# A graph-attention layer on one Trainium2 core: adjacency loads of 2 MB in four buffers instead of 1 MB in six, and TensorE packing whole tiles behind each step's other work

## What is computed

```python
x   = normal(8192, 256)                       # float32
adj = bernoulli(0.000488281, (8192, 8192))    # int32
h = maximum(layernorm(x), 0)
support = (h @ weight)                        # 4 heads of 64
f1, f2  = einsum(support, weight_u), einsum(support, weight_v)
scores  = leaky_relu(f1[None, :] + f2[:, None], 0.2) * adj     # 0 where there is no edge
attn    = softmax over the nonzero entries of a row
out     = x + attn @ support + bias + h @ proj_w.T + proj_b
```

## Time and profile before

| what | value |
|---|---|
| time, median of 3 runs | 862.98 us (861.75 to 863.88) |
| time of the profiled execution | 860.12 us |
| its span, first to last instruction | 858.4 us |
| busy PE, PEld, DVE, ACT, POOL | 83%, 51%, 75%, 15%, 62% |
| DMA traffic | 329.82 MB, mean 384 GB/s |
| of it adjacency | 256 transfers of 1024 KB, median 13.3 us from issue to landing |
| of it gathers | 384, median 6.2 us from issue to landing |
| chain that ended last | PE 42%, DMA 25%, DVE 24% |

### The profile page before, as it was taken

How to read it: one execution, slowest core, us unless ns; L and a number is a source line. 1 busy time by engine, 2 the same in 40 slices (tenths; PEclk the granted TensorE clock), 3 DMA queues, 4 the chain that set the end, 5 groups by cost and what they waited for, 6 DMA issues and landing times.

```text
span 858.4 us, 11157 instructions
## 1 busy us (share of the span) xinstructions
PE 710.9 (83%) x3011; PEld 434.2 (51%) x3011; DVE 643.1 (75%) x2740; ACT 129.3 (15%) x467; POOL 529.0 (62%) x598
## 2 busy tenths in 40 slices
PE   2989999999956878887888888788888878888865
PEld 0656666666513545454555445354544445454454
DVE  4556666657446988879869798977979787886887
ACT  0223333333210111000001011000011100000010
POOL 4344455454467776667766667676766766676570
PEclk9999999999966989888879898887989888988789
DMA  9999999999999999999999999999999999999971
GB/s 307 422 407 393 416 422 416 407 423 413 419 410 384 385 401 402 388 405 384 402 393 374 399 374 405 383 404 384 390 396 375 406 366 400 359 403 401 397 302 53
DMA packets 63855, 329.82 MB, mean 384 GB/s; under 512 B 12795, under 2 KB 15560, under 8 KB 31024
## 3 DMA queue, kind: packets, MB, share of 16 engines
q1 hardware_dynamic: 43056, 286.28, 83.8%
q0 software_dynamic: 18432, 34.30, 11.1%
q10 hardware_dynamic: 2304, 8.52, 2.4%
HBM read 328.99 MB, written 16.91 MB: 403 GB/s over the span
## 4 chain that ended last, share of the span: by engine, by line
PE 42%; DMA 25%; DVE 24%; issue 4%; POOL 3%; ACT 1%; POOLq 0%; ACTq 0%; SPq 0%
DMA adj_raw<-in_adj 21%; PE ps_words L400 11%; PE ps_agg L461 9%; PE ps_agg L381 7%; PE ps_two L381 6%; DVE att L933 5%; PE ps_two L400 5%; DVE cand L787 3%; DVE base L943 3%; POOL att L717 2%; DMA att<-support_table,idx 2%; PE ps_score L445 2%; DMA att<-in_x 1%; PE ps_words L392 1%; DMA support_table<-att 1%
## 5 line engine op out<-in xcount | busy, mean ns | idle before, releaser
L717 POOL DMA_INDIRECT att<-support_table,idx x384 | 417.4, 1087 | 188.7 <-issue 105.8
L400 PE MATMUL ps_words<-adj_raw,pack_w 128*128 128x512 fp8e4 x640 | 186.7, 428 | 25.4 <-DMA adj_raw<-in_adj 25.3
L461 PE MATMUL ps_agg<-att,ident 128*128 128x260 f32 x640 | 176.3, 428 | 8.5 <-DVE att L933 8.5
L461 PEld LDWEIGHTS ps_agg<-att,ident 128*128 128x128 f32 x640 | 135.1, 218 | 41.6 <-issue 18.6
L400 PE MATMUL ps_two<-adj_raw,pack_w 128*128 128x512 fp8e4 x384 | 118.9, 457 | 24.6 <-DMA adj_raw<-in_adj 24.5
L400 PEld LDWEIGHTS ps_words<-adj_raw,pack_w 128*128 128x128 bf16 x640 | 62.1, 106 | 125.3 <-DMA adj_raw<-in_adj 39.8
L787 DVE MAX8 cand<-ps_words 128x8 f32<-128x128 f32 x320 | 67.1, 281 | 66.3 <-PE ps_words L400 66.3
L933 DVE TENSOR_TENSOR att<-att 128x1536 f32<-128x1536 f32 x64 | 109.4, 1750 | 0.4 <-ACT att L625 0.4
L708 POOL COPY record<-att 128x8 f32<-128x8 f32 x64 | 13.4, 209 | 117.4 <-ACT att L569 117.4
L400 PEld LDWEIGHTS ps_two<-adj_raw,pack_w 128*128 128x128 bf16 x384 | 38.7, 113 | 91.5 <-DMA adj_raw<-in_adj 40.0
L381 PE MATMUL ps_agg<-w_all,hT 128*128 128x260 f32 x256 | 63.0, 389 | 4.1 <-ACT hT L565 4.1
(11 more groups left out here) (118 smaller groups left out, 821.2 us busy)
## 6 DMA issues: line engine op xcount, KB each, us to landing
adj_raw<-in_adj SPq DMA_DIRECT2D x256, 1024.0 KB, 13.3
support_table<-att ACTq DMA_DIRECT2D x16, 520.0 KB, 8.8
att<-in_x SPq DMA_DIRECT2D x16, 512.0 KB, 6.7
out<-base SPq DMA_DIRECT2D x15, 512.0 KB, 14.1
att<-support_table,idx POOLq DMA_INDIRECT x384, 6.2
out<-base SPq DMA_DIRECT2D x4, 128.0 KB, 1.9
w_all<-in_proj_wT SPq DMA_DIRECT2D x2, 128.0 KB, 6.0
w_all<-in_weight SPq DMA_DIRECT2D x2, 128.0 KB, 6.3
```

Of the source, the lines that this page charges most:

```text
L400: mm = nc.tensor.matmul(ps_words[buffer_of(t)][:, k * 512:(k + 1) * 512], pack_w[:, u * UT + s, :], adj_low[:, n % HELD, s, k * 512:(k + 1 ...
L461: mm = nc.tensor.matmul(ps_agg[:, b, 0:ROW], ident[:] if k < OWN else onehotT[:, g % RING, b], gathered[:, g % RING, b, k], start=(k == 0) ...
L717: pool.indirect_dma_start(gathered[:, g % RING, b, k, :], None, table, bass.IndirectOffsetOnAxis(idx[:, g % RING, b, k:k + 1], 0), bounds_ ...
```

## The change

Five things change, and all arithmetic stays.

- UNITS goes from 4 to 2 and HELD from 6 to 4. A tile's adjacency comes in two transfers of 2 MB, 16 KB in one piece for each partition, and 8 MB are held instead of 6. A unit's packing is now eight matmuls, and the buffer is freed behind the eighth.
- In the first phase the two units of a tile are packed in the second and the fourth place of a round, eight matmuls each, in place of four in each of four places.
- In a step of the second phase TensorE first runs `offsets`, `aggregate`, `edge_records`, `row_scores`, `aggregate` and `edge_refs`, and packs in one go behind them.
- It packs tile t + 2 in the step that picks t. Tile 17 is packed ahead of the first step; tile 63 keeps its place in the step behind the loop.
- To make room in SBUF, `spare`, `uv_row`, `projb_row` and `place_hi` become views of `base`, and `hT` a view of `onehot`. These are used at other times than what they now share with.

```diff
-UNITS = 4
-HELD = 6
+UNITS = 2
+HELD = 4
@@ tiles
-        spare = sb("spare", [P, 4, HF])
-        uv_tmp = spare[:].rearrange("p (q c) d -> p q c d", q=2)
+        uv_tmp = base[:, TILES - 4:].rearrange("p (q c) d -> p q c d", q=2)
+        uv_row = base[:, TILES - 6:TILES - 4]
+        projb_row = base[:, TILES - 7]
+        place_hi = base[0:2, TILES - 9:TILES - 7].rearrange("p a d -> p (a d)").bitcast(BF16)
-        hT = sb("hT", [P, 2, KC * P])
+        hT = onehot[:].rearrange("p a b m -> p a (b m)")
@@ first phase
-                    if q > 0:
-                        pack_unit(g + 1, q - 1)
+                    if q > 0 and q % (LOAD // UNITS) == 0:
+                        pack_unit(g + 1, q // (LOAD // UNITS) - 1)
@@ second phase
             pe.wait_ge(s_staged, TILES)
+            pack_places(FIRST + 1)
+            for u in range(UNITS):
+                pack_unit(FIRST + 1, u)
             for g in range(LATE):
-                new = [t + 1 for t in picks[g]]
                 offsets(g)
-                pack_places(new[0])
-                for u in range(UNITS // 2):
-                    pack_unit(new[0], u)
                 if g >= 2:
                     aggregate(g - 2, 0)
                 edge_records(g)
                 if g > 0:
                     row_scores(g - 1)
-                for u in range(UNITS // 2, UNITS):
-                    pack_unit(new[0], u)
-                if g > 0:
-                    edge_refs(g - 1)
                 if g >= 2:
                     aggregate(g - 2, 1)
-                for t in new[1:]:
-                    pack_places(t)
-                    for u in range(UNITS):
-                        pack_unit(t, u)
+                if g > 0:
+                    edge_refs(g - 1)
+                for t in picks[g]:
+                    if t + 2 < TILES - 1:
+                        pack_places(t + 2)
+                        for u in range(UNITS):
+                            pack_unit(t + 2, u)
```

## The result

| kernel | median us | lowest to highest | ratio to before [95%] |
|---|---|---|---|
| before | 863.13 (6 runs) | 858.91 to 863.88 | |
| changed | 911.23 (6 runs) | 907.81 to 915.66 | 1.0569 [1.0547, 1.0592] |

The changed kernel is 5.7% slower. The forecast was 886 us with a range up to 903: the right sign and the right cause, with half of the size. The profiled execution of the changed kernel took 915.66 us, its span is 913.8 us. So the two spans differ by 55.4 us where the medians differ by 48.1.

What follows compares the result with a forecast made beforehand. The second phase was taken as DMA-bound at 37.7 us a pair, becoming gather-paced at 39.8. 13 pairs gave +27, the start +3, the end -7: +23 us, so a median of 886 us, range 838 to 903.

Steps and rivals of the forecast that it cites:

- The mechanism: Second phase: 16 KB rows lengthen q1's turns, so a gather takes 1.95 us against 1.3 us of issue, and VectorE waits.
- with the chain first this wait goes: VectorE's waits for `edge_rec`, 51.2 us in all, vanish once TensorE runs its chain ahead of packing.
- 11.9 + 27.9 = 39.8 us: Second-phase pair of steps: 11.9 us from `scores` to first gather issue plus a 27.9 us burst, against 37.7 now.
- my own 1.95: Engine time taken for one gather beside 16 KB rows, between 1.90 and 2.11 us; it gave a 28.3 us burst.
- The discount of 8/9 for semaphore packets: One q1 packet in nine is a semaphore update costing no turn, so a gather takes at least 1.90 us.
- The start: Second phase's beginning: first burst up to 6.4 us longer, partly before q1 is full, and tile 17 packed ahead: +3 us.
- The end: Step from 784.96 to 811.74 took 26.8 us against 19.9; loads ahead of the chain remove the excess: -7 us.
- The faster rival: DMA gaps close and gathers still fit, pair at 36.2 us, median 841 us; chance 0.29.
- unchanged: More held data and the order bring nothing since DMA is full, gathers keep 3.8 us slack: 863 us; chance 0.09.
- a fixed 2 us: Skill page's cost per transfer, by which halving adjacency loads would save 256 us; taken as hidden by the queue.
- The slower rival: Packs in one go at the lower clock delay the next step's `offsets`; pair 42.0 us, 915 us; chance 0.07.
- I book 0: TensorE's new order and packing two tiles ahead in the second phase: added waits cost nothing, VectorE having 2 us to spare.

Runs made afterwards that it cites:

- size_only: The changed kernel's 2 MB units and four buffers, but TensorE's second phase in the order of the kernel before: 929.23 us, 1.0786 of before.
- order_six: The changed kernel's TensorE order and packing two tiles ahead, with the loads of the kernel before (1 MB, 8 KB rows, six held): 867.7 us, 1.0064 of before.
- order_eight: The changed kernel with 1 MB units, 8 KB rows and eight held, same 8 MB and same order: 867.55 us, 1.0069 of before.
- late_start: The changed kernel with tile 17 packed behind the first step's chain in the second phase, not ahead of offsets(0): 920.02 us, 1.0542 of before.
- before_eight: The kernel before, old order and 1 MB loads, with eight buffers held instead of six: 872.39 us, 1.0039 of before.
- two_loads: The changed kernel with each 2 MB unit fetched in two 1 MB loads of 8 KB rows: 867.72 us, 1.0051 of before.
- two_start: As two_loads, but with tile 17 packed behind the first step's chain: 866.17 us, 1.0061 of before.

## Why the forecast was off

*The mechanism held.* Gathers paced by q1's longer turns, one packet of each; VectorE waiting every other step; the loop "12 us from `scores` to the first issue, and then the burst". 12.0 us were measured for 11.9. Gathers took 9.5 us (9 to 13 forecast), the share was 0.90 as forecast, 361 GB/s for 370, and q1's packets fell from 22185 to 10229 in 485 us. The other group's gathers do come through in the gap. The Trainium skill, "DMA: Bandwidth & Descriptors", section "Queues, rings and completion order", has 9 to 17 descriptors to a turn; 258 packets against 260 again say one row.

*Two signs came true for another reason.* The `edge_slot` wait shrank from 51.2 to 4.1 us, and TensorE's weight loads wait 5.4 us for the adjacency of `ps_two` where they waited 40.0. The forecast gave both to the new order and the larger lead. But in size_only, which has the long rows and the old order, they are as short, so they go without the new order:

```profile
DVE edge_slot L868 <- ACT edge_rec L620: 3.6, 3, 2.2
...
PEld ps_two L400 <- DMA adj_raw<-in_adj: 3.3, 2, 2.1
```

With the new order and short rows 25.4 us of `edge_slot` waits are left in order_six and 24.8 in order_eight, and 73.7 and 35.8 us of TensorE's for `ps_two`. So "with the chain first this wait goes" failed where it could be tested.

*The burst was mis-sized, and with it the pair: 41.28 for 39.8.* This is the step that failed: the term "27.9" in "11.9 + 27.9 = 39.8 us". It measured 29.4 us here and 29.2 in the median of groups 5, 7, ... 27, and I had set it below even the 28.3 us of my own 1.95. The price of one gather wasn't wrong. In those twelve bursts q0's 48th packet (three for each of 16 engines, so the first gather's number) starts 6.5 us after the first issue, and its 576th (the twelfth's) at 27.4 us: (27.4 - 6.5) / 11 = 1.90 us a gather, the lower end of the forecast. What it left out is the end. `scores` can read only 1.8 us behind that packet. From 712 to 738 us q0 has 618 packets, 42 more than the burst's 576, so the next group's gathers were already running on some engines while the last one of this group was still out. I read this as `scores` waiting for the last engine, where the sum counts the mean of sixteen; the profile doesn't name the engine of a packet, so that part stays open. The discount of 8/9 for semaphore packets holds (230 of 258). Times 13 the pair's 1.5 us are 19 us, the largest part of the miss.

*The start: +8.8 us for +3* (`scores` of group 2 at 303.6 for 294.8). The step that failed is that part of the first burst comes "before q1 is full again". size_only, with the old order, issues its first gather at 239.5 us as before, and reads it at

```profile
267.89 0.20 DVE L886 TENSOR_TENSOR score<-att,record 128x40 f32<-128x40 f32 x1 [20.52 <-DMA att<-support_table,idx]
```

28.4 us later, for 20.6 before (first issue at 239.5, read at 260.05): nearly 8 us at once. Tile 17's place, which I had counted in, makes the first `scores` of the changed kernel another 3.5 us late (late_start), and nothing of that is left by group 2. The new order with six buffers makes group 2 late by 2.1 us (the table); with eight it is 4.5, but before_eight, with the old order and eight buffers, is as late (299.8 us, on another chip), so the rest needn't be the order. Beside the long rows the order adds 1.2 (303.6 for 302.4).

*The end: +0.2 us for -7* (from `scores` of group 28 to the span's end 73.6 us for 73.4). It is two things. The steps of groups 28 to 31 did get shorter, 51.9 us for 56.1, with the long one at 20.9 for 26.8; size_only has 20.9 too, so it isn't the order that shortens it. The last stretch then ran at a lower clock, here beside the last 22 us of the kernel before (columns as in the earlier trace rows; before stands second):

```profile
890.00:912.00 22.00, 16.81 (x59) 13.25 (x59) 13.53 (x48) 0.34 (x2) 0.00 (x0) 0.77 0.12 43
```

```profile
835.00:857.00 22.00, 13.71 (x68) 10.93 (x66) 17.21 (x64) 0.67 (x4) 1.89 (x2) 1.00 0.16 56
```

The granted clock is 0.77, where before had 1.00. Two executions of one kernel differ by the same 4 us at this place, and thirteen of sixteen profiled executions have the longer end, size_only, order_six and before_eight among them. So I put it down to the execution and not to the change, and the profiled one of the kernel before was among the rarer ones. Then the change gave back 4 us at the end, not 7, and 4.4 of the 55.4 us between the profiles are chance.

*Check of the sum.* 13 x 3.57 + 8.8 + 0.2 = 55.4 us, where 27 + 3 - 7 = 23 were forecast.

*The faster rival had no room.* It was given 0.29 for 841 us, from the floor of 35.8 us. two_loads, order_six, order_eight and two_start are that rival made real, with short rows and every other part of the change: 866 to 868 us, pairs of 37.9 to 38.0. The premise, gaps that 8 MB would fill, was wrong: the share of 1.00 in the earlier trace rows said that there were none. The chance should have gone to "unchanged", at 863 us.

*A page read wrongly.* The forecast has "a fixed 2 us" to each transfer from the section "Bandwidth". The Trainium skill, "DMA: Bandwidth & Descriptors", states it in "Anatomy of one DMA — SWDGE (gpsimd) path", and both it and the 78% are for transfers that GpSimd issues; the adjacency loads are SP's. No sum rested on it.

*The slower rival* gave the right number, 915 us, for a reason that is half absent. Its 2.11 us a gather is close to the measured 2.05. The packs at the lower clock are not there: TensorE's timeline of the changed kernel has them at full speed, sixteen matmuls in 3.8 us, where eight took 3.62.

```profile
704.30 3.77 PE L400 MATMUL ps_two<-adj_raw,pack_w 128*128 128x512 fp8e4 x16
708.54 3.78 PE L400 MATMUL ps_words<-adj_raw,pack_w 128*128 128x512 fp8e4 x16
```

And *"I book 0"* for the order was wrong with short rows: order_six is 0.6% slower than before, with `offsets` behind packs that wait for loads.

No version beat the kernel before.

## What to carry to other kernels

When a queue of small indirect transfers shares the DMA engines with bulk loads, as here, the bulk load's row length sets the small one's latency: count the small queue's packets on an engine, multiply by the time of one bulk row, and compare with the rate of issue, before making the rows longer. That gives the rate; the last landing came another 1.8 us behind it here. Take the time of a row from a stretch in which both queues run, and take a DMA share of 1.00 at its word: more buffers don't help it. A reordering that brings a chain forward on an engine also puts the next link of that chain behind what was moved back.

## What the chip showed that I had not expected

- Gathers that move almost nothing cost almost as much latency as full ones: 27.6 us for 29.4 in a burst.
- An 8 KB row took 0.31 us alone and 0.331 us in the mean beside gathers, a 16 KB row 0.64. That 7% was the whole of the gap that I had meant to close.
- TensorE's clock over the last 20 us differs between executions of one kernel, and is worth 4 us of 865.
- The last of a load's sixteen increments came 6.8 us behind the fifteenth in order_eight and 0.6 us in order_six, and the pair of steps was 37.9 and 38.0 us.
- One chip gave 1.05 to a kernel that has 1.007 on another, with the kernel before about 1% apart on the two (871.0 and 862.1 us).
